# Inverted residual stage: all blocks' second channel set on VectorE, the 32 remaining channels on GpSimd

## What is computed

```
h = relu(bn1(einsum('oc,bchw->bohw', w1, x)))        # 48 -> 288 channels
h = relu(bnd(depthwise 3x3 convolution of h, wd))    # 288 channels, padding 1
h = bn2(einsum('oc,bchw->bohw', w2, h))              # 288 -> 48 channels
return x + h
```

## Time and profile before

| | us |
|---|---|
| median of 3 runs | 2010.66 (2002.27 to 2011.61) |
| the profiled execution, its own time | 2013.56 |
| its span from first to last instruction | 2011.8 |
| inverted residual: first depthwise matmul to the end of the span | 1570.1 to 2011.8 |
| mean granted TensorE clock over the span | 0.926 |

### The profile page before, as it was taken

One profiled execution on the slowest core, in us unless ns is written; L12 is line 12 of the kernel. 1 busy time (PEld: TensorE's weight loads), 2 busy tenths in 40 slices (PEclk: granted clock), 3 DMA queues, 4 the chain that ended last, 5 costly groups with the idle time before them and its releaser, 6 DMA issues. The chain is left out here.

```text
span 2011.8 us, 41164 instructions
## 1 busy us (share of the span) xinstructions
PE 1595.3 (79%) x13002; PEld 940.3 (47%) x13002; DVE 1479.1 (74%) x2699; ACT 1171.4 (58%) x2257; POOL 637.3 (32%) x577
## 2 busy tenths in 40 slices
PE   6979418888888888803888888888860899999997
PEld 5545215555555555302555555555520344444444
DVE  5548858888888888654888888888856766666666
ACT  1115207888888888642888888888853434444341
POOL 2010015555555555302555555555500000000000
PEclk9999659999999999856999999999985799999999
DMA  2759356666666666565666666666576011011100
GB/s 64 251 201 217 93 135 105 107 106 107 107 108 107 107 106 103 97 144 130 106 107 106 108 106 107 106 106 107 85 119 161 15 34 34 21 31 34 34 18 25
DMA packets 132266, 199.40 MB, mean 99 GB/s; under 512 B 28528, under 2 KB 47824, under 8 KB 131920
## 3 DMA queue, kind: packets, MB, share of 16 engines
q1 hardware_dynamic: 132176, 198.08, 52.8%
HBM read 73.72 MB, written 37.75 MB: 55 GB/s over the span
## 5 line engine op out<-in xcount | busy, mean ns | idle before, releaser
L719 PE MATMUL gates_l<-xh_l,w_l 128*112 128x512 f32 x3072 | 801.2, 410 | 124.4 <-ACT xh_l L756 124.2
L719 PEld LDWEIGHTS gates_l<-xh_l,w_l 128*112 128x112 f32 x3072 | 502.8, 176 | 421.9 <-issue 286.5
L683 POOL TENSOR_TENSOR xh_l<-hs,xh_l 48x512 fp32r<-48x512 f32 x252 | 299.9, 1190 | 444.8 <-ACT xh_l L756 444.8
L692 POOL TENSOR_TENSOR xh_l<-xf_l,xs_l 48x512 fp32r<-48x512 f32 x256 | 307.1, 1200 | 47.8 <-DVE xs_l L825 47.4
L719 PE MATMUL gates_l<-xc_l,w_l 128*112 128x512 f32 x512 | 164.9, 403 | 143.0 <-DMA xc_l<-xs_l 135.8
L849 DVE TENSOR_TENSOR hs<-gate_o_l,tanh_c_l 48x256 f32 (+1 forms) x512 | 193.3, 416 | 73.9 <-ACT tanh_c_l L785 70.1
L1289 PE MATMUL b_dw<-b_hid,b_diag 32*32 32x512 f32 x6840 | 235.5, 601 | 0.0
L785 ACT ACTIVATE tanh_c_l<-cell_l 48x256 f32<-48x256 f32 x512 | 158.1, 342 | 99.2 <-DVE cell_l L840 99.2
L775 ACT ACTIVATE gate_if_l<-gates_l 112x512 f32<-112x512 f32 x256 | 151.3, 591 | 105.0 <-PE gates_l L719 101.8
L840 DVE TENSOR_TENSOR cell_l<-keep_l,gates_l 48x512 f32<-48x512 f32 x256 | 178.5, 697 | 26.6
L836 DVE TENSOR_TENSOR gates_l<-gate_if_l,gates_l 48x512 f32<-48x512 f32 x256 | 178.4, 697 | 22.3 <-ACT gates_l L779 1.0
(11 more groups left out here) (150 smaller groups left out, 1457.0 us busy)
## 6 DMA issues: line engine op xcount, KB each, us to landing
xc_l<-xs_l SPq DMA_DIRECT2D x512, 99.0 KB, 3.0
xh_l<-xs_l SPq DMA_DIRECT2D x512, 66.0 KB, 2.4
xf_l<-rows SPq DMA_DIRECT2D x256, 96.0 KB, 2.2
hs<-rows SPq DMA_DIRECT2D x32, 384.0 KB, 9.9
rows<-hs SPq DMA_DIRECT2D x32, 384.0 KB, 5.1
xr<-in_x_rows SPq DMA_DIRECT2D x24, 256.0 KB, 2.7
xc<-in_x_cols SPq DMA_DIRECT2D x24, 256.0 KB, 2.9
mixed<-stage SPq DMA_DIRECT2D x24, 256.0 KB, 3.0
```

Of the source, the lines that this page charges most:

```text
L683: pool.tensor_tensor(inner(xh[n:n + C, d, 1 - s, LO, :]), whole, inner(xh[n:n + C, d, 1 - s, HI, :]).bitcast(F32), ALU.subtract).then_inc( ...
L692: pool.tensor_tensor(inner(xh[f:f + C, d, s, HI, :]), wide(xf[f:f + C, s, :]), inner(x_rows(s, slice(f, f + C))).bitcast(F32), ALU.subtrac ...
L719: return nc.tensor.matmul(ps[d][m][0:K, :], w[:, d, q, m, :], padded(tile)[:, :, lo:lo + W], start=first, stop=last)
```

## The change

Set 1 goes to DVE in all blocks but the last (`on_dve` is true for g == 1 and k + 1 < NBLK), so `depthwise(k, 1)` stays on PE in block 15 alone. `acc_v` becomes two buffers, used in turn. `begin_v(k+1)` moves to the end of ACT's iteration k, ahead of `squash_v(k)`, which opens iteration k+1. The rest of 32 channels leaves DVE for GpSimd, whose taps are each two instructions: a tensor_scalar into one of two new buffers `tap_r`, and a tensor_tensor add into `acc_r`. The scaling of tap n+1 is issued ahead of the addition of tap n. `squash_rest` moves to GpSimd too.

```diff
-        acc_v = sb("b_acc_v", [P, BLK * B, W])
+        acc_v = [sb(f"b_acc_v{i}", [P, BLK * B, W]) for i in range(2)]
+        tap_r = sb("b_tap_r", [P, 2, BLK * QB, W])
...
         def on_dve(k, g):
-            return g == 1 and k % 2 == 0
+            return g == 1 and k + 1 < NBLK
...
                     if on_dve(k, 1):
-                        pe.wait_ge(squashed_v, k // 2 + 1)
+                        pe.wait_ge(squashed_v, k + 1)
...
                 for k in range(2):
                     for n in range(EPB):
                         keep(k, n, (0,))
+                begin_v(0)
                 for k in range(NBLK):
                     more = k + 2 < NBLK
-                    if on_dve(k, 1):
-                        begin_v(k)
-                    elif k:
+                    if k:
                         squash_v(k - 1)
                     squash(k, 0)
...
+                    if k + 1 < NBLK and on_dve(k + 1, 1):
+                        begin_v(k + 1)
+
+            @block.gpsimd
+            def _(pool):
+                pool.wait_ge(pads, 8)
+
+                def taps(k):
+                    ahead = EPB * (min(k + 1, NBLK - 1) + 1) - 1
+                    pool.wait_ge(kept_a, by_act(ahead))
+                    pool.wait_ge(kept_d, by_dve(ahead))
+
+                    def scaled(n, dst):
+                        dy, dx = ORDER[n]
+                        src = hid_r[:, BLK * k + 1 + dy:BLK * k + 1 + dy + BLK, :, dx:dx + W].rearrange("p r b w -> p (r b) w")
+                        return pool.tensor_scalar(dst, src, wds[:, 2, 3 * dy + 3 + dx:3 * dy + 4 + dx], None, ALU.mult)
+                    if k:
+                        pool.wait_ge(squashed_r, k)
+                    scaled(0, acc_r[:, :, :]).then_inc(taps_r, 1)
+                    scaled(1, tap_r[:, 1, :, :]).then_inc(scaled_r, 1)
+                    for n in range(1, 9):
+                        if n < 8:
+                            if n > 1:
+                                pool.wait_ge(taps_r, 9 * k + n)
+                            scaled(n + 1, tap_r[:, (n + 1) % 2, :, :]).then_inc(scaled_r, 1)
+                        pool.wait_ge(scaled_r, 8 * k + n)
+                        pool.wait_ge(taps_r, 9 * k + n)
+                        pool.tensor_tensor(acc_r[:, :, :], acc_r[:, :, :], tap_r[:, n % 2, :, :], ALU.add).then_inc(taps_r, 1)
...
                 for k in range(NBLK):
-                    taps(k, range(9))
-                    squash_rest(k)
                     if on_dve(k, 1):
                         taps_set(k, range(0, 3))
                     if k:
                         finish(k - 1, 0)
```

More of the change, by code:

```diff
@@ L1171, in inverted_residual @@
         squashed_v = sem("b_squashed_v")
+        scaled_r = sem("b_scaled_r")
         taps_r = sem("b_taps_r")
@@ L1362, in begin_v @@
                 def begin_v(k):
-                    ahead = EPB * (k + 1) + 3
+                    ahead = EPB * k + 3
                     act.wait_ge(kept_a, by_act(ahead))
@@ L1366, in begin_v @@
                     src = hid[1][:, BLK * k % RING:BLK * k % RING + BLK, :, 1:1 + W].rearrange("p r b w -> p (r b) w")
-                    nc.scalar.activation(acc_v[:, :, :], src, ACT.Copy, scale=wds[:, 1, 4:5]).then_inc(begun_v, 1)
+                    nc.scalar.activation(acc_v[k % 2][:, :, :], src, ACT.Copy, scale=wds[:, 1, 4:5]).then_inc(begun_v, 1)
                 def squash_v(k):
-                    act.wait_ge(taps_v, 8 * (k // 2) + 8)
-                    nc.scalar.activation(h2[:, k % 2, 1, :, :].rearrange("p r n -> p (r n)"), acc_v[:, :, :].rearrange("p r w -> p (r w)"),
+                    act.wait_ge(taps_v, 8 * k + 8)
+                    nc.scalar.activation(h2[:, k % 2, 1, :, :].rearrange("p r n -> p (r n)"), acc_v[k % 2][:, :, :].rearrange("p r w -> p (r w)"),
                                          ACT.Relu, bias=bias_r[:, 1:2]).then_inc(squashed_v, 1)
@@ L1391, in _, with squash_rest @@
                         keep(k + 2, 4, (0, 1))
+                    if k + 1 < NBLK and on_dve(k + 1, 1):
[23 more added lines that the diff above has]
+                        pool.tensor_tensor(acc_r[:, :, :], acc_r[:, :, :], tap_r[:, n % 2, :, :], ALU.add).then_inc(taps_r, 1)
+                def squash_rest(k):
+                    if k >= 2:
+                        pool.wait_ge(reduced, 2 * k - 2)
+                    pool.wait_ge(taps_r, 9 * k + 9)
+                    pool.tensor_scalar(h2_r[:, k % 2, :, :].rearrange("p r n -> p (r n)"),
+                                            acc_r[:, :, :].rearrange("p r w -> p (r w)"), bias_d[:, 2:3], 0.0,
+                                            ALU.add, ALU.max).then_inc(squashed_r, 1)
+                for k in range(NBLK):
+                    taps(k)
+                    squash_rest(k)
             @block.vector
@@ L1413, in _ @@
                     keep(n // EPB, n % EPB)
-                dve.wait_ge(pads, 8)
+                dve.wait_ge(pads, 6)
                 def taps_set(k, some):
@@ L1423, in taps_set @@
                             dve.wait_ge(kept_d, by_dve(ahead))
-                            dve.wait_ge(begun_v, k // 2 + 1)
+                            dve.wait_ge(begun_v, k + 1)
                         else:
-                            dve.wait_ge(taps_v, 8 * (k // 2) + n)
+                            dve.wait_ge(taps_v, 8 * k + n)
                         for at, slot, rows in pieces(k, dy):
                             src = hid[1][:, slot:slot + rows, :, dx:dx + W].rearrange("p r b w -> p (r b) w")
-                            part = acc_v[:, at * B:(at + rows) * B, :]
+                            part = acc_v[k % 2][:, at * B:(at + rows) * B, :]
                             nxt = nc.vector.scalar_tensor_tensor(part, src, wds[:, 1, 3 * dy + 3 + dx:3 * dy + 4 + dx], part, ALU.mult, ALU.add)
                         nxt.then_inc(taps_v, 1)
[L1433 to L1457, removed]
                 def finish(k, p):
```

## The result

| | before | after |
|---|---|---|
| median, us (runs) | 2008.38 (4: 2002.27 to 2011.61) | 2187.75 (4: 2179.58 to 2191.8) |
| profiled execution: own time, span, us | 2013.56, 2011.8 | 2191.8, 2190.0 |
| mean granted TensorE clock | 0.926 | 0.879 |

The change makes the kernel slower: ratio 1.0888, with a 95% interval of 1.085 to 1.0926. The forecast of 1960 us and the range up to 2070 both missed it.

The account below looks back on a forecast made before the run. PE was taken as the bound. Blocks 1 to 13 at 310.1 instead of 360.1 us, plus 0.9 in the tail, took 50.9 off 2013.56: 1962.7, stated as 1960 after a 2.9 run offset; 8-in-10 range 1938 to 2070.

Parts of the forecast that it names:

- PE, ACT and DVE: Blocks 1 to 13: PE sets the pace at 23.7 us a block, DVE's 20.5 us fits, ACT's added wait is hidden.
- The dip in every block: Low TensorE clock during block 6's sparse reduction matmuls, costing 1.65 us, priced into every block.
- The stall at the last block: In the tail, PE's 6.24 us wait for block 14's squash_v was to shrink by only 0.9 us.
- The 0.25 us for a tap cut at the ring's end: DVE's last three taps, where cut into pieces: some 0.25 us more per piece pair, 0.75 in all.
- GpSimd's price: GpSimd's rest: scalings at 0.85 us, additions at 1.19, 19.6 us a block, under PE's 23.7.
- GpSimd is the bound: Rival, 9%: slower scalings make GpSimd's block set the pace; centred on 2015 us, a third each side of no change.
- The overlap: DVE's and GpSimd's taps side by side through the last stage, priced at no mutual delay.
- the pair at 298 us: ConvLSTM trace: DVE's L833 and a GpSimd addition overlapped 0.55 us at usual lengths; taken as evidence against exclusion.
- full exclusion: Rival, 16%: DVE's 18.8 us of taps and GpSimd's 19.6 queue, 38.4 us a block, about 2170 us in all.
- the cast row: Trace: a one-source DVE cast issued during GpSimd's 13.74 us memset took 10.96 us; taken as evidence for exclusion.
- Once the shares that exclude each other add up to more than 27.7 us: Condition under which full exclusion decides against the change; 27.7 us is the mean block before.
- The clock: Rival, 5%: low TensorE clock lasts through the sparse part, 32 us a block, 2066 us in all.

Follow-up runs that it names:

- e2: The changed kernel with GpSimd's taps 2 to 9 of the rest left out, one scaling and the squash kept: 1951.74 us, ratio 0.9721 to the kernel before.
- e1: The changed kernel with DVE's eight set 1 taps replaced by one-input sums over image columns: 2015.52 us, ratio 1.0039 to the kernel before.
- m1: A separate kernel, computing nothing of the reference, timing single DVE and GpSimd instructions alone and in overlapping pairs: a scaling alone takes 1.56 us.

## Why the prediction was wrong

The way from 2008 to 2188 us, by runs that each leave one cost out:

| step | us | runs |
|---|---|---|
| depthwise(k, 1) off PE, the rest off DVE | -57 | before 2008, e2 1952 |
| GpSimd's own pace | +64 | e2 1952, e1 2015.5 |
| GpSimd and DVE excluding each other | +172 | e1 2015.5, after 2188 |

Against the forecast of 1960 that is 8 us less on PE's side, 64 more for GpSimd's pace and 172 more for the overlap. (e1 has sums of one input in place of DVE's taps, of nearly the same length.)

- *PE, ACT and DVE: right.* The kernel without GpSimd's taps was to take 1960 and takes 1952. Blocks of 23.64 and 21.99 us, taps of 2.34, no wait for ACT's squash_v in the block. The dip in every block was the term that was too large: six of thirteen blocks of e2 are without it. The stall at the last block was to shrink from 6.24 to about 5 us; in e2 PE stood for 5.81 (1918.91 to 1924.72), so 0.4 of the 0.9 was won. The 0.25 us for a tap cut at the ring's end doesn't follow from the working beside it, which gives 0.16 (0.744 + three quarters of 2.345 - 2.345); the pieces measured 1.81 and 0.75 against 2.35, which is 0.21. It weighs next to nothing in the sum.
- *GpSimd's price: right in mechanism, wrong in size.* "I take 0.85" for a scaling; it is 1.56. The squash, counted as a tenth scaling, is 2.00. The additions are 1.27 against 1.19. The block is 27.1 us instead of 19.6. The bounds of 0.48 and 2.1 held it; the choice between them did not. I leaned on "it reads one tensor instead of two", but the addition with two inputs is the cheaper one. The slope of 3.6 ns an element from the small tensor_scalars, which I set aside, was nearer the truth: 1.56 less 0.24 over 512 is 2.6 ns. Those small instructions each carry two operations, as the squash does, and for the squash the slope nearly holds: 2.00 less 0.24 over 512 is 3.4 ns. The rival "GpSimd is the bound" is what e1 measures; that its centre of 2015 is e1's time to the microsecond is luck, since it was the middle of a wide guess.
- *The overlap: the step that failed.* The term "So I price the overlap at nothing" measured 172 us, 11.7 a block. It rested on the pair at 298 us, read as an instruction with two SBUF inputs. A row names tensors and not their memory. In the code of the ConvLSTM the second input, `cell`, is made with `psum_tensor` (L573). So the trace of before held no VectorE instruction with two SBUF inputs beside GpSimd at all, and nothing in it spoke against the rival "full exclusion"; the cast row, of one source, showed at least that VectorE can be held. I named the holes in that reading ("these are short") and missed the one that mattered. m1 shows both: 48 x 512 with both inputs in SBUF is delayed, a tap with its second input in PSUM delays nobody.
- *The rival "full exclusion": this is nearly what happened,* with 2170 forecast and 2188 measured, and 38.4 us a block against 38.8. That the block agrees is luck, since two errors cancel. GpSimd's share is 27.1 and not 19.6, and a strict queue of 18.8 and 27.1 would give 45.9. The hand-overs are cheaper than that: between 1763.43 and 1803.13 four scalings take 1.91 us longer each and four additions 1.15 to 1.51, 12.6 in all, and 27.1 + 12.6 is the 39.7 that lies between these squashes.
- *"Once the shares that exclude each other add up to more than 27.7 us"* was the right condition but the milder half of it: GpSimd alone was already at 27.1, so any delay of it went straight into the block.
- *The clock: not the cause, by the chain.* It fell to 0.79 in the stage, but PE holds 2% of the chain; with PE's waits shorter it is back over the span, to 0.912 in e1 and 0.922 in e2.

Of the signs named ahead, the one given for exclusion is there (additions and taps longer, ends one behind the other), and so is the one for GpSimd as the bound (PE waiting in `reduce_main` for its squash).

## What to carry to other kernels

Before an overlap of VectorE and GpSimd is priced from a row, look up in the code in which memory each operand lies: the row doesn't say, and a tap with its second input in PSUM costs GpSimd nothing where one in SBUF cost it up to 2.1 us. Price GpSimd by an instruction of the same kind and size run by itself, since a two-input addition does not bound a scaling from above. And when an engine takes work over, compare its own block with the block of before first, and its neighbours' interference only after that.

## What the runs showed of the hardware

- GpSimd multiplies 128 x 512 fp32 by a per-partition scalar in 1.56 us and adds two such tensors in 1.26; an addition of a scalar followed by a maximum takes 2.00. The Trainium skill (GPSIMD Engine Reference, section Elementwise — side-by-side cycle accounting) has 0.77 us for 512 elements of a tight loop, its best case; tensor_scalar here takes twice that.
- The exclusion isn't symmetric. An addition on GpSimd that started first held a VectorE tap for 0.89 us (3.24 against 2.35), nearly its whole remainder of 1.08; a scaling that started first held the tap for only 0.33 (2.68), though the scaling still had 1.42 to run. So the prediction's "for the whole instruction" doesn't hold for it. A VectorE instruction with two SBUF inputs that started first held the GpSimd scaling or addition in every pair of m1. Why a scaling holds the tap so much less no run here shows.
- An instruction that is held counts as busy: of GpSimd's 38.8 us a block 11.7 were spent so, and its busy share was 97% (513 of 528).
